# Context keys taken from raw rows, their norms computed among the decoder layers, turned rows loaded by DMA

## The reference, cut to what matters

```python
x = x + L0_xattn(...)    # 4 decoder layers, 16 heads: self-attention, cross-attention to the first 32 context rows, gated FFN
x = x + L0_attn(...)     # pairwise messages with factors u and v
x = x + L0_ffn(...)
x = x + L1_xattn(ctx, layernorm(x), mask, ...)
x = x + L1_attn(...)     # a fifth rope attention
x = x + L1_ffn(...)      # 8 experts, the best 2 of each token

def L1_xattn(x, latents, mask, ...):          # x: context [8,1601,128]; 2 heads of 64
    xn, ln = layernorm(x, ln_x_g, ln_x_b), layernorm(latents, ln_l_g, ln_l_b)
    q = ln @ W_q
    k, v = split(concat([xn @ W_kv, ln @ W_kv], axis=1))
    sim = (rmsnorm(q) * q_gamma * 64 ** -0.5) @ (rmsnorm(k) * k_gamma).T
    sim = where(mask padded with True, sim, -max)
    return softmax(sim) @ v @ W_out + b_out
```

## Time and profile before

| | |
|---|---|
| runs | 491.57, 495.98, 493.18 us; median 493.18 |
| profiled execution | 495.46 us, its span 493.5 us, mean granted clock 0.972 |
| instructions | 14858 |
| DMA | 10321 packets, 27.84 MB, 16 engines busy 16.1% in the main queue |

### The profile page before, as it was taken

How to read it: one execution, slowest core, us unless ns; L and a number is a source line. 1 busy time by engine, 2 the same in 40 slices (tenths; PEclk the granted TensorE clock), 3 DMA queues, 4 the chain that set the end, 5 groups by cost and what they waited for, 6 DMA issues and landing times.

```text
span 493.5 us, 14858 instructions
## 1 busy us (share of the span) xinstructions
PE 455.0 (92%) x5683; PEld 392.6 (80%) x5705; DVE 366.1 (74%) x1053; ACT 280.3 (57%) x752; POOL 217.8 (44%) x350
## 2 busy tenths in 40 slices
PE   8998998999879989999789999978999899999997
PEld 3666876777769767889779899867889798789996
DVE  5888899669874897565752669978788996865553
ACT  3688487767766787662562544836657644443131
POOL 4703474534452475211652449966667751110000
PEclk9999799999988998999989999979999999999999
DMA  7921222030201400000420037030100000000000
GB/s 206 386 83 41 68 79 66 3 107 20 98 30 35 139 3 2 2 3 3 149 70 1 4 114 298 17 117 2 68 2 2 0 1 1 3 1 4 0 2 26
DMA packets 10321, 27.84 MB, mean 56 GB/s; under 512 B 1391, under 2 KB 5381, under 8 KB 9990
## 3 DMA queue, kind: packets, MB, share of 16 engines
q1 hardware_dynamic: 10246, 26.82, 16.1%
HBM read 26.55 MB, written 0.26 MB: 54 GB/s over the span
## 4 chain that ended last, share of the span: by engine, by line
PE 58%; DVE 20%; POOL 8%; ACT 6%; issue 6%; DMA 1%; SPq 0%; DVEq 0%; POOLq 0%; ACTq 0%
PE ps L1164 6%; PE ps L1155 6%; PE ps L1008 3%; PE ps L1094 3%; PE ps L939 3%; PE ps L879 3%; PE ps L1079 3%; PE ps L972 2%; POOL rk L1739 2%; PE ps L869 2%; PE ps L1067 2%; DVE mx L1381 2%; POOL rsx L1720 2%; PE ps L999 2%; DVE own L1386 2%
## 5 line engine op out<-in xcount | busy, mean ns | idle before, releaser
L1682 POOL TENSOR_TENSOR rstd<-ss,par 128x1 f32<-128x1 f32 x52 | 28.7, 557 | 60.0 <-ACT sq L1184 59.9
L1739 POOL TENSOR_TENSOR rk<-rk,par 128x8 f32<-128x8 f32 (+1 forms) x32 | 46.0, 1438 | 2.7
L1212 ACT ACTIVATE own<-own 128x512 f32<-128x512 f32 x56 | 35.2, 628 | 17.4 <-DVE own L1412 8.7
L1381 DVE TENSOR_REDUCE mx<-ps 128x8 f32<-128x512 f32 x40 | 27.3, 682 | 5.0 <-PE ps L861 4.7
L1079 PE MATMUL ps<-own,xnT 128*128 128x128 f32 x208 | 29.6, 282 | 0.9 <-DVE ssq L1486 0.3
L1164 PE MATMUL ps<-we,own 128*128 128x128 f32 x256 | 30.3, 276 | 0.0
L1672 POOL TENSOR_TENSOR qk<-own 128x128 f32<-128x128 f32 x40 | 18.6, 470 | 25.9 <-DVE own L1374 25.4
L1164 PEld LDWEIGHTS ps<-we,own 128*128 128x128 f32 x256 | 29.7, 192 | 0.4
L1155 PE MATMUL ps<-hT,we 128*128 128x256 f32 x128 | 29.7, 381 | 0.2 <-issue 0.2
L1079 PEld LDWEIGHTS ps<-own,xnT 128*128 128x128 f32 x208 | 28.5, 197 | 1.4 <-issue 0.5
L1342 ACT ACTIVATE own<-ps,we 128x256 f32<-128x256 f32 x32 | 13.4, 470 | 28.4 <-PE ps L1155 22.5
(11 more groups left out here) (247 smaller groups left out, 1309.0 us busy)
## 6 DMA issues: line engine op xcount, KB each, us to landing
cx<-ctx_in SPq DMA_DIRECT2D x14, 768.0 KB
we<-we_in SPq DMA_DIRECT2D x8, 514.0 KB, 6.8
wc<-wc_in SPq DMA_DIRECT2D x4, 768.5 KB, 6.0
wa<-wa_in SPq DMA_DIRECT2D x5, 387.0 KB, 3.0
uvT<-uvT_in SPq DMA_DIRECT2D x1, 1024.0 KB, 10.1
uv<-uv_in SPq DMA_DIRECT2D x1, 1024.0 KB, 10.5
wb<-wb_in SPq DMA_DIRECT2D x4, 128.5 KB, 4.2
wm<-wm_in SPq DMA_DIRECT2D x1, 512.0 KB, 6.0
```

Source lines behind the costliest of these rows:

```text
L1212: done(nc.scalar.activation(pr[:, g, a:a + 512], sd[:, g, a:a + 512], ACT.Exp), p)
L1381: done(nc.vector.tensor_reduce(mx[:, g, 8 * k:8 * k + 8].rearrange("p (r i) -> p r i", i=4), quad(od, i, g)[:, 2 * k:2 * k + 2, :, :], AX, ...
L1682: done(nc.gpsimd.tensor_tensor(rstd[:, t:t + 1], ss[:, t:t + 1], par[:, 1:2], ALU.pow), p)
L1739: done(nc.gpsimd.tensor_tensor(rk[:, n, 0:2 * w], rk[:, n, 0:2 * w], par[:, 1:2].to_broadcast([P, 2 * w]), ALU.pow), p)
```

## The change

- The context rows are no longer centred. c_turn, c_turned and the subtraction of c_normed go; c_normed and c_spread scale the raw rows in place in `cx` (three buffers now, pitch 130 elements). The mean's removal and the layernorm's gain go into the weights, made once (w_centre, w_bias into `wcen`, `bconst`).
- The turned rows come from the host's layout of the context (`keyT_in`) by DMA, eight times 0.85 MB (13 tiles of 128 x 128 f32) into `xTe` for the keys and eight times into `xT` for the scores.
- Offset and mask are added by one bf16 product per group, for the keys (`sel` by `rowsT`, new) and for the scores (`selq` by `rowsT`, in place of `sel` by `notm`). `rowsT` is a product per sample (c_rows) of a block `stg` that c_power fills on POOL, now with nine operations of 128x13 to 128x39 instead of four. `selq` is made by POOL per sample (sel_q, 128x1664); `sel` itself is multiplied once on DVE (k_split, 128x1664). The query products of qk0 and qk1 get a second half (weights `wcen`), and q_bias (8 products) with q_biased and q_split is new.
- c_keys, c_squares, c_sums and c_rnorm are done in the order of the samples among the layers. The maximum of c_rnorm goes to DVE, into c_sums.
- On SP, `load_keys` brings the weights and `sel` in the opening. `load_sample` loads rows and `xTe` and waits for c_keys of two samples earlier too. `load_rest` waits for the last sample's keys, and loads `sel` again and four samples' `xT` from there.
- ACT's m_tanh waits for the last sample's c_keys and c_rnorm, since `qh` shares memory with `xTe`.
- PLACES, PLACED and WARM are written anew; the fillers count 30 instead of 29 (the first piece has 8 instead of 7).

The table of places, as an example of its rows, and the core of the diff:

```diff
-    "c_keys": (395, 405, 429, 435, 439, 440, 441, 444, 454, 455, 456, 462, 480, 493, 494, 502, 516, 518, 528, 531, 538, 542, 556, 558, 564, 566, 574,
+    "c_keys": (345, 349, 351, 353, 367, 369, 372, 377, 101, 107, 112, 114, 135, 142, 145, 150, 162, 176, 185, 194, 196, 206, 213, 220, 251, 276, 283,
```

```diff
-            elif p == "c_turn":
-                bank = take(pe, od, p, i, g)
-                if g < 2:
-                    after(pe, od, "c_normed", i, g)
-                else:
-                    after(pe, od, "c_spread", i, g - 2)
+            elif p == "c_rows":
+                bank = take(pe, od, p, i, g)
+                after(pe, od, "x_consts", 0)
+                after(pe, od, "c_power", i)
+                done(nc.tensor.matmul(bank[:, 0:P], stg[STATS.index(i) % 2][:], identb[:], start=True, stop=True), p)
+            elif p == "c_keys":
+                bank, m = take(pe, od, p, i, g), STATS.index(i)
+                after(pe, od, "w_taken", 0)
+                after(pe, od, "k_split", 0)
+                after(pe, od, "c_rows_taken", i)
+                pe.wait_ge(s["key_loaded%d" % (m % 2)], 16 * (m // 2 + 1))
+                nc.tensor.matmul(bank[:, 0:P * width(g)], rowsT[:, i, :], sel[:, c_tiles(g), :], start=True, stop=True)
                 for j, c in enumerate(CG[g]):
-                    last = nc.tensor.transpose(bank[:, P * j:P * j + P], xh[i % 3][:, c, 0:D], ident)
-                done(last, p)
-            elif p == "c_keys":
-                bank = take(pe, od, p, i, g)
-                after(pe, od, "c_turned", i, g)
-                for j, c in enumerate(CG[g]):
-                    last = nc.tensor.matmul(bank[:, P * j:P * j + P], xnT[n % 3][:, P * j:P * j + P], xw[:, X_K:X_K + P], start=True, stop=True)
+                    last = nc.tensor.matmul(bank[:, P * j:P * j + P], xTe[m % 2][:, P * c:P * c + P], wcen[:, 0:P], start=False, stop=True,
+                                            skip_group_check=True)
                 done(last, p)
             elif p == "c_scores":
                 bank = take(pe, od, p, i, g)
-                after(pe, od, "c_turned", i, g)
+                after(pe, od, "c_rows_taken", i)
+                after(pe, od, "sel_q", i)
...
-                nc.tensor.matmul(bank[:, 0:w], notm[:, i, :], sel[:, P * CG[g][0]:P * CG[g][0] + w], start=True, stop=True)
+                pe.wait_ge(s["turned_loaded%d" % k], 16 * (t + 1))
+                nc.tensor.matmul(bank[:, 0:P * width(g)], rowsT[:, i, :], selq[k][:, c_tiles(g), :], start=True, stop=True)
                 for j, c in enumerate(CG[g]):
-                    last = nc.tensor.matmul(bank[:, P * j:P * j + P], xnT[n % 3][:, P * j:P * j + P], columns(qp[t][:, k, :, :]),
-                                            start=False, stop=True, skip_group_check=True)
+                    last = nc.tensor.matmul(bank[:, P * j:P * j + P], xT[k][:, P * c:P * c + P], columns(qpc[t][:, k, :, :]), start=False,
+                                            stop=True, skip_group_check=True)
                 done(last, p)
...
                 after(pe, od, "weights", i, g)
+                if g < 2:
+                    after(pe, od, "c_normed", i, g)
+                else:
+                    after(pe, od, "c_spread", i, g - 2)
...
             elif p in ("m_tanh0", "m_tanh1"):
                 w = int(p[-1])
                 after(act, od, "m_sums%d" % (1 - w), i - 2)
+                after_all(act, od, "c_keys", STATS[-1])
+                after_all(act, od, "c_rnorm", STATS[-1])
                 after(act, od, "m_pairs%d" % w, i)
...
-                after(act, od, "c_turn", i, g)
-                done(nc.scalar.activation(xnT[n % 3][:, 0:w], held(od, "c_turn", i, g)[:, 0:w], ACT.Identity, scale=xw[:, X_GX:X_GX + 1],
-                                          bias=xw[:, X_BX:X_BX + 1]), p)
...
+                m = 4 * STATS.index(i) + g - 1
+                if m >= 0:
+                    after(act, od, "c_sums", STATS[m // 4], m % 4)
...
+            elif p == "k_split":
...
+                done(nc.vector.tensor_tensor(sel[:], sel[:], kp[:].unsqueeze(1).to_broadcast([P, CT, P]), ALU.mult), p)
...
             elif p == "c_sums":
                 after(dve, od, "c_squares", i, g)
-                done(nc.vector.tensor_reduce(kss[:, n, 0:2 * w], ksq[n % 2][:, 0:P * w].rearrange("p (a d) -> p a d", d=XD), AX, ALU.add), p)
+                after(dve, od, "c_power", i)
+                squares = kss[:, n, 0:2 * w]
+                step(dve, "vector_step", nc.vector.tensor_reduce(squares, ksq[:, 0:P * w].rearrange("p (a d) -> p a d", d=XD), AX, ALU.add))
+                squares = squares.rearrange("p (c h) -> p c h", h=XH)
+                done(nc.vector.tensor_tensor(squares, squares, flx[:, i, c_tiles(g)].unsqueeze(2).to_broadcast([P, w, XH]), ALU.max), p)
...
             elif p == "c_power":
...
+                    after(pool, od, "c_rows", STATS[m - 2])
+                pool.wait_ge(s["xw_loaded"], 48)
                 after_all(pool, od, "c_moments", i)
-                step(pool, "pool_step", nc.gpsimd.tensor_tensor(rsx[:, i, :], mvx[:, i, :, 1], par[:, 0:1].to_broadcast([P, CT]), ALU.add))
-                step(pool, "pool_step", nc.gpsimd.tensor_tensor(rsx[:, i, :], rsx[:, i, :], par[:, 1:2].to_broadcast([P, CT]), ALU.pow))
-                step(pool, "pool_step", nc.gpsimd.tensor_tensor(mrx[:, i, :], mvx[:, i, :, 0], rsx[:, i, :], ALU.mult))
-                done(nc.gpsimd.tensor_scalar(mrx[:, i, :], mrx[:, i, :], -1.0, None, ALU.mult), p)
+                nc.gpsimd.tensor_scalar(rows[:, 0:CT], mraw[:, i, :], -1.0, 1.0, ALU.mult, ALU.add)
+                step(pool, "pool_step", nc.gpsimd.tensor_tensor(vex[:], mvx[:, i, :, 1], par[:, 0:1].to_broadcast([P, CT]), ALU.add))
+                step(pool, "pool_step", nc.gpsimd.tensor_tensor(rsx[:, i, :], vex[:], par[:, 1:2].to_broadcast([P, CT]), ALU.pow))
+                nc.gpsimd.tensor_scalar(flx[:, i, :], vex[:], RMS_FLOOR, None, ALU.mult)
+                step(pool, "pool_step", nc.gpsimd.tensor_tensor(sdx[:], vex[:], rsx[:, i, :], ALU.mult))
+                step(pool, "pool_step", nc.gpsimd.tensor_copy(parts(0, 3), spread(sdx, 3)))
+                step(pool, "pool_step", nc.gpsimd.tensor_tensor(rex[:], sdx[:], rows[:, CT:2 * CT], ALU.subtract))
+                step(pool, "pool_step", nc.gpsimd.tensor_copy(parts(3, 2), spread(rex, 2)))
+                done(nc.gpsimd.tensor_tensor(rows[:, 6 * CT:7 * CT], rex[:], rows[:, 4 * CT:5 * CT], ALU.subtract), p)
             elif p == "c_normed":
-                shape, tiles = [P, w, D], c_tiles(g)
-                part = xh[i % 3][:, tiles, 0:D]
-                if i >= 3:
...
-                    after(pool, od, "x_clear", 0)
+                tiles = c_tiles(g)
+                part = cx[i % 3][:, tiles, 0:D]
                 after(pool, od, "c_power", i)
+                pool.wait_ge(s["ctx_loaded%d" % (i % 3)], rows_loaded(i))
+                done(nc.gpsimd.tensor_tensor(part, part, rsx[:, i, tiles].unsqueeze(2).to_broadcast([P, w, D]), ALU.mult), p)
+            elif p == "sel_q":
+                if leads(od, p, i, g):
+                    pool.wait_ge(s["late_loaded"], 48)
                 if i >= 2:
-                    pool.wait_ge(s["ctx_loaded%d" % (i % 2)], 32 * (B // 2 + i // 2))
-                step(pool, "pool_step", nc.gpsimd.tensor_tensor(part, cx[i % 2][:, tiles, :], mvx[:, i, tiles, 0].unsqueeze(2).to_broadcast(shape),
-                                                                ALU.subtract))
-                done(nc.gpsimd.tensor_tensor(part, part, rsx[:, i, tiles].unsqueeze(2).to_broadcast(shape), ALU.mult), p)
+                    after_all(pool, od, "c_scores", i - 2)
+                after(pool, od, "q_split", i // 2)
+                done(nc.gpsimd.tensor_tensor(selq[i % 2][:], cp[:, i // 2, i % 2, :].unsqueeze(1).to_broadcast([P, CT, P]), sel[:], ALU.mult), p)
             elif p == "c_rnorm":
                 after(pool, od, "c_sums", i, g)
-                step(pool, "pool_step", nc.gpsimd.tensor_scalar(rk[:, n, 0:2 * w], kss[:, n, 0:2 * w], RMS_FLOOR, None, ALU.max))
-                done(nc.gpsimd.tensor_tensor(rk[:, n, 0:2 * w], rk[:, n, 0:2 * w], par[:, 1:2].to_broadcast([P, 2 * w]), ALU.pow), p)
+                done(nc.gpsimd.tensor_tensor(rk[:, n, 0:2 * w], kss[:, n, 0:2 * w], par[:, 1:2].to_broadcast([P, 2 * w]), ALU.pow), p)
...
         def load_sample(sp, od, n):
             if n >= 2:
                 after_all(sp, od, "c_moments", STATS[n - 2])
+                after_all(sp, od, "c_keys", STATS[n - 2])
             else:
                 after(sp, od, "x_zero", n)
-            load_batch(sp, STATS[n])
...
+            sp.dma_start(xTe[n % 2][:], keyT_in[STATS[n]]).then_inc(s["key_loaded%d" % (n % 2)], 16)
...
+        def load_context(sp, od, b):
+
+            if b >= 2:
+                after_all(sp, od, "c_scores", b - 2)
```

(66 more changed lines are left out.)

724 lines of the change are left out of this document (380 added, 344 removed), and 50 rows, old and new, of the table PLACES.

## The result

The changed kernel takes 504.91 us (median of three runs, 503.05 to 506.63) where the kernel before takes 493.18: **slower, by a ratio of 1.027 (95% interval 1.022 to 1.032)**. The forecast was 478, with a range of 456 to 500. Its profiled execution took 503.05 us, with a span of 501.1.

The account below looks back on a forecast made before the run. PE's filling and its interruptions were taken to bound the kernel. Profiled 495.46 us, + 30.6 (layers), - 42.8 and - 2.6 (the rest), gave 480.7, or 478 us at the median's level; range 456 to 500.

Parts of the forecast that it names:

- PE's total: PE's busy time over the whole kernel: 18.2 us added against 16.0 removed, so it does not fall, staying near 457.
- What is removed: Context-row turns, 16.0 us of PE; their copies, 18.2 us of ACT; one POOL pass over half the rows, about 17.6 us.
- The layers, +30.6: Decoder layers, 20 to 206 us: 36.7 us of added PE work, partly filling idle time, lengthens them to 216.6 us.
- my 95: PE's busy share assumed in the lengthened layers, in percent: the middle between today's 90.9 and 100.
- I take nothing for it: Context stage: selq on POOL holding up DVE operations counted as 0 us, since fewer passes and 46.0 us of powers leave.
- the bound, 28.7 us: Context stage: each selq could hold DVE for 3.6 us, at most 28.7 us in all, an estimate.
- What the rest gets back, -45.4: From 206 us on: PE falls to 228.1 us, at 93.2% share 244.7, so -42.8; waits that go, -2.6.
- DVE loses only the key sums: Context stage: DVE keeps scaling, maxima and shifts, falling from 113.6 to 95 us, so it shrinks less than PE.
- Costed at nothing: Items counted as 0: first turned rows and second `sel` (6 to 7 us if late), late layer loads, DMA queue, clock.
- POOL's order: Layers: key powers in POOL's queue ahead of layer norms' powers; room in sum, 142 of 217 us, order left to a rival.
- The clock: Two 20 us stretches in the layers at granted clock 0.83; giving all back is worth 6.8 us, none counted.
- The slower one: Rival: POOL's powers fall on the layers' path, layers take 55 us more, 503 us; chance 0.16.

Follow-up runs that it names:

- the run without keys: Changed kernel with the key stage in the layers cut to one 128x128 mask product per group, POOL's powers and all transfers kept: 505.1 us, ratio 1.027.
- the run with added powers: Changed kernel with POOL's selq cut to 128x128 and two powers, 128x13 and 128x4, ahead of each, keeping the path as long: 486.4 us, 0.989.
- the run in 13 pieces: Changed kernel with each selq on POOL made in 13 operations of 128x128 instead of one of 128x1664: 492.0 us, ratio 1.000.
- the small selq: Changed kernel with POOL's selq cut from 128x1664 to 128x128, score products taking the plain selection block: 486.0 us, ratio 0.986.
- cheap key powers: Changed kernel with the keys' powers on POOL (1.65 us each) replaced by same-shape products (some 0.22 us): 502.1 us, ratio 1.016.

## Why the prediction was wrong, step by step

- **PE's total** does not fall: right, 455.5 us. **What is removed** went as costed.
- **The layers, +30.6.** In the window that the forecast gave them, PE did 203 of 206 us of work. The share, 93.6% against my 95, was near, and the layers end 31 us later. But a clock of 1.00 in place of 0.95 helped, which I had counted at nothing, and in the run without keys 15 us less work of PE moved the end of the layers by 4.4 us only. The sum fits; my reason for it is not shown, so that some of the fit may be luck, and what sets the layers stays open.
- **The step that failed: "I take nothing for it"**, of DVE held up by selq. I had the bound, 28.7 us, beside it; with all of it the sum would have been 478 + 28.7 = 507 us, and 505 was measured. That these two are so near is luck: the hold lengthened DVE by 15.7 us and cost 19 us of time, and 8 us are due to something else. I set it off against the passes and powers that leave the stage. That was wrong twice: the powers never held DVE up (in the kernel before, the 15 maxima of 128x256 that overlap one took 417 to 427 ns, and in the run with added powers 16 took 409 to 426), and the passes' holds, 1.1 us at most, were covered. A hold of 3.3 us was not: it fell on the maxima between the scores and the shift, and PE waited for what stands behind them in DVE's queue, as from 386 us on. Without it the time is 19 us less. The rule of the Trainium skill that I quoted (SBUF — State Buffer, SBUF: two separate sides), a hold for the whole of GpSimd's instruction, agrees with the 3.47 us of a 0.43 us maximum and with the run in 13 pieces; for powers the traces here don't bear it out.
- **What the rest gets back, -45.4.** Measured -23.0 (264.5 against 287.5). With the small selq the second stretch took 247.9 us against my 242.1, and with the added powers 242.6, in an execution of 481.1 us at a clock of 0.988: the term held, within 6 us, but for the hold. "DVE loses only the key sums" missed the hold and the four operations of the query's split a tile, 6.1 us in all.
- **Costed at nothing**: loads, right as far as tested (expert weights later, no change); POOL's order, not quite (some 1%, 5 us, with cheap key powers). The clock: I said it could give back up to 6.8 us. It rose in the layers, 0.95 to 1.00, and fell behind them, 0.98 to 0.94, where PE's waits came.
- **The rivals.** The slower one has the right time, 503, by the wrong mechanism: it had POOL's powers delay the layers. None of mine had POOL delay DVE.
- **What is left.** 486.0 with the small selq stands 8 us above 478. Short POOL operations don't bring it. It is not settled. POOL's key powers may hold part of it: cheap ones gave some 5 us, and in the small-selq run's chain of work that ended last three of them stand end to end (start us, us), ahead of a power that the message stage needs:

```profile
225.40 4.81 POOL rk L1843 x3
```

  That this is the missing part is argued and not shown; the clock may have another part.
